# Latent experts weighted by the square root of the gate, and the kept experts with eight buffers

## The reference

```
# layer 0, latent mixture: 32 experts, 8 of them per token
wsel = take(scores, topi); wsel = wsel / wsel.sum(-1) * 2.5
cw = zeros((T, 32)).at[token, topi].add(wsel)       # gate of each token and expert, never negative
x_lat = x @ fc1_w.T                                 # T x 128
h = relu2(einsum('tl,eil->eti', x_lat, w1))         # 32 x T x 128
h = h * cw.T[:, :, None]
routed = einsum('eti,eli->tl', h, w2) @ fc2_w.T
# layer 1, kept experts: 48, each takes at most 96 tokens
gu = einsum('ech,eoh->eco', xb, gate_up_proj); g, u = split(gu)
out = einsum('eci,ehi->ech', silu(g) * u, down_proj)
final = zeros_like(x).at[tok].add(out[...] * w)
```

## Time and profile before

| | |
|---|---|
| time, median of 3 runs | 3288.59 us (3288.56 to 3289.65) |
| the profiled execution | 3292.41 us, of which the span from first to last instruction is 3290.7 us |
| PE, PEld | busy 2926.5 us (89%), 2298.1 us (70%) |
| DVE, ACT, POOL | busy 1834.3 us (56%), 1582.4 us (48%), 704.0 us (21%) |
| DMA | 125.69 MB, 39 GB/s over the span |
| routing phase | 892 to 952 us of the span |
| latent experts | 952 to 1398 us |
| kept experts | 3080 to 3262 us, then the last additions to the end |

### The profile page before, as it was taken

The page is one execution under the profiler, slowest core; times in us unless marked ns, Lnnn a source line. Parts: engine busy times, 40 slices in busy tenths (PEclk is TensorE's granted clock), DMA queues, the critical chain, the costliest instruction groups (busy, mean ns, idle before and its releaser), DMA issues. The chain is left out here.

```text
span 3290.7 us, 52269 instructions
## 1 busy us (share of the span) xinstructions
PE 2926.5 (89%) x17936; PEld 2298.1 (70%) x17936; DVE 1834.3 (56%) x3318; ACT 1582.4 (48%) x2917; POOL 704.0 (21%) x735
## 2 busy tenths in 40 slices
PE   5699999959849999969999999999999999958584
PEld 4544444358737777658888888888888888857453
DVE  5388888451177777755555555555555554555321
ACT  5247777744149999843333333333333333324110
POOL 2412222100120000012222222222222222204564
PEclk7789999979679999979999999999999999965555
DMA  4865554000010000000000000000000000031366
GB/s 148 230 94 79 73 74 67 5 15 0 14 40 0 0 0 0 0 20 10 10 6 3 10 10 10 10 10 10 10 10 10 4 6 10 8 109 56 89 145 125
DMA packets 149298, 125.69 MB, mean 38 GB/s; under 512 B 16960, under 2 KB 134240, under 8 KB 148640
## 3 DMA queue, kind: packets, MB, share of 16 engines
q1 hardware_dynamic: 140752, 109.47, 15.1%
q0 software_dynamic: 8448, 14.99, 2.5%
HBM read 82.55 MB, written 46.06 MB: 39 GB/s over the span
## 5 line engine op out<-in xcount | busy, mean ns | idle before, releaser
L744 DVE TENSOR_REDUCE score_pm<-score_SM 128x1 f32<-128x512 f32 (+3 forms) x608 | 364.5, 658 | 122.8 <-PE score_SM L613 72.9
L1399 POOL TENSOR_TENSOR lin_o2sum<-lin_o2sum,lin_o 128x512 f32<-128x512 f32 x128 | 165.6, 1294 | 1047.3 <-ACT lin_o L1435 1047.3
L704 ACT ACTIVATE score_PR<-score_SE 128x512 f32<-128x512 f32 (+1 forms) x640 | 310.5, 559 | 105.1 <-PE score_SE L638 101.7
L1614 DVE SCALAR_TENSOR_TENSOR lin_go<-lin_gT,lin_O 128x512 f32<-128x512 f32 x128 | 88.0, 688 | 477.7 <-ACT lin_o L1435 477.7
L1470 PE MATMUL lin_PJ<-C_XH,lin_WH 128*128 128x512 f32 x1032 | 341.7, 412 | 13.1 <-DVE lin_WL L1574 13.1
L1470 PE MATMUL lin_PJ<-C_XH,lin_WL 128*128 128x512 f32 x1032 | 320.5, 392 | 0.0
L1470 PE MATMUL lin_PJ<-C_XL,lin_WH 128*128 128x512 f32 x1032 | 320.3, 392 | 0.0
L1418 ACT ACTIVATE lin_qT<-lin_PJ 128x512 f32<-128x512 f32 x129 | 77.2, 598 | 378.3 <-PE lin_PJ L1470 378.3
L1631 DVE TENSOR_TENSOR lin_acc<-lin_OUT,lin_acc 128x512 f32<-128x512 f32 x256 | 177.1, 692 | 140.2 <-PE lin_OUT L1505 138.8
L610 PE MATMUL score_SM<-score_KR,score_QR 96*128 96x512 bf16 (+3 forms) x768 | 230.3, 341 | 27.7 <-DMA score_V<-v_rows 25.0
L1241 DVE TENSOR_TENSOR experts_h<-experts_sq,experts_CW 128x512 f32<-128x512 f32 x256 | 176.2, 688 | 92.7 <-ACT experts_sq L1155 92.6
(11 more groups left out here) (343 smaller groups left out, 6708.4 us busy)
## 6 DMA issues: line engine op xcount, KB each, us to landing
score_QR<-q_parts SPq DMA_DIRECT2D x96, 128.0 KB
score_KR<-k_parts SPq DMA_DIRECT2D x96, 128.0 KB
kept_GU<-L_ffn_gate_up_proj SPq DMA_DIRECT2D x48, 192.0 KB
v_rows<-qkv_vt SPq DMA_DIRECT2D x32, 256.0 KB, 2.6
score_V<-v_rows SPq DMA_DIRECT2D x16, 512.0 KB
C_w<-L_attn_w_qkv SPq DMA_DIRECT2D x51, 128.0 KB, 2.3
q_parts<-qkv_parts SPq DMA_DIRECT2D x16, 384.0 KB, 2.7
k_parts<-qkv_parts SPq DMA_DIRECT2D x16, 384.0 KB, 2.6
```

The lines of the kernel that those rows point to most:

```text
L704: nc.scalar.activation(PR[:, st % BUFS, h, 0:width], SE[:, e % RING, 0:width], ACT.Exp, scale=SCALE)\
L744: nc.vector.tensor_reduce(pm[:, n % 2, h0:h0 + nh, t, k0 // CHUNK], SM[:, count % RING, 0:nh * nk].rearrange("p (h k) -> p h k", h=nh), AX ...
```

## The change

Three parts.

**Roots in place of gates.** Since the gate c is not negative, relu(a)^2 * c = (max(a, 0) * sqrt(c))^2. The routing phase now ends in sqrt(w): a floor at 1e-30, ACT's square root, one Newton step on DVE (a reciprocal, two elementwise operations, and one that also multiplies by the selection mask), 32 fp32 transposes, and a copy. The result (32 x 4096) is stored to a tensor in HBM, `B_roots`. `pick`, its matmul, `CW` and the bf16 parts are gone. In the expert phase SP loads the roots of four experts and one chunk to all 128 partitions at once (`sq`, 128 x 4 x 512 fp32, the source repeated for every partition), four such buffers in turn.

**Another pipeline for the latent experts.** DVE makes z = max(HP, 0) * root in one instruction; ACT squares z twice, once to fp32 and once to fp32r; the low part is made by DVE, and for every fourth expert by POOL. `HP`, `h`, `hh`, `hl` have four buffers, `Y` two (so chunks alternate), the fc2 products are issued behind experts 4 and 7.

**Kept experts.** Eight buffers in place of six, and PE's transposes go one expert further ahead.

The core of the diff (lines that only go away are in the listing above):

```
@@ group_routing_phase @@
-def group_routing_phase(nc, a, scores, CWT, identb, W1H, W1L, W2H, W2L, pick):
+def group_routing_phase(nc, a, scores, roots, ident, W1H, W1L, W2H, W2L):
...
-        TB = ph.ps("TB", [CWR, 4, 1024], BF16)
+        TB = ph.ps("TB", [E, 4, 2 * CHUNK])
...
+            for j in range(4):
+                sp.wait_ge(copied, j + 1)
+                cols = slice(j * 2 * CHUNK, (j + 1) * 2 * CHUNK)
+                sp.dma_start(roots[:, cols], rootT[:, cols]).then_inc(stored, 16)
+            sp.wait_ge(stored, 64)
...
-            nc.gpsimd.memset(pick[:], 0.0).then_inc(zero, 1)
-            pool.wait_ge(zero, 1)
-            for j in range(TERMS):
-                rows = pick[j * E:(j + 1) * E]
...
-            pool.wait_ge(picked, TERMS)
             for n, (w, e) in enumerate(LOADS):
...
-            step(nc.vector.tensor_copy(parts[:, :, 0, :], w[:]))
-            step(tt(rest[:], w[:], parts[:, :, 0, :], ALU.subtract))
-            step(nc.vector.tensor_copy(parts[:, :, 1, :], rest[:]))
-            tt(parts[:, :, 2, :], rest[:], parts[:, :, 1, :], ALU.subtract).then_inc(parts_ready, 1)
+            nc.vector.tensor_scalar(root[:], w[:], 1.0e-30, None, ALU.max).then_inc(positive, 1)
+            dve.wait_ge(rooted, 1)
+            step(nc.vector.reciprocal(inv[:], root[:]))
+            step(tt(inv[:], inv[:], w[:], ALU.mult))
+            step(tt(inv[:], inv[:], root[:], ALU.add))
+            nc.vector.scalar_tensor_tensor(root[:], inv[:], 0.5, left[:], ALU.mult, ALU.mult).then_inc(roots_ready, 1)
...
-            pe.wait_ge(parts_ready, 1)
+            pe.wait_ge(roots_ready, 1)
             for t in range(TILES):
-                ins = nc.tensor.transpose(TB[:, t // 8, (t % 8) * P:(t % 8 + 1) * P],
-                                          parts[:, t].rearrange("p s e -> p (s e)"), identb[:])
+                ins = nc.tensor.transpose(TB[:, t // 8, (t % 8) * P:(t % 8 + 1) * P], root[:, t, :], ident[:])
...
+            act.wait_ge(positive, 1)
+            nc.scalar.activation(root[:], root[:], ACT.Sqrt).then_inc(rooted, 1)
             for j in range(4):
                 act.wait_ge(transposed, j + 1)
-                nc.scalar.activation(CWT[:, j * 1024:(j + 1) * 1024], TB[:, j], ACT.Copy).then_inc(copied, 1)
-
+                nc.scalar.activation(rootT[:, j * 2 * CHUNK:(j + 1) * 2 * CHUNK], TB[:, j], ACT.Copy).then_inc(copied, 1)
@@ experts_phase @@
-    SLOTS = 3
+    QE = 4
+    NQ = E // QE
+    BUFS = 4
+    COPY_AT, OUT_AFTER, ADD_AT = 2, (4, 7), (7, 10)
...
+        sq = ph.sb("sq", [P, BUFS, QE, CHUNK])
+        z = ph.sb("z", [P, 2, CHUNK])
+        h = ph.sb("h", [P, BUFS, CHUNK])
+        hh = ph.sb("hh", [P, BUFS, CHUNK], F32R)
+        hl = ph.sb("hl", [P, BUFS, CHUNK], F32R)
         y = ph.sb("y", [P, CHUNK])
+        HP = ph.ps("HP", [P, BUFS, CHUNK])
+        Y = ph.ps("Y", [P, 2, CHUNK])
         OP = ph.ps("OP", [P, 2, D])
...
+        def on_pool(e):
+            return e % 4 == 3
...
+            def load(g, q):
+                src = roots[q * QE:(q + 1) * QE, bass.ds(g * CHUNK, CHUNK)]
+                sp.dma_start(sq[:, q % BUFS], src.rearrange("(o e) n -> o e n", o=1).to_broadcast([P, QE, CHUNK]))\
+                    .then_inc(sq_in[q % BUFS], 16)
+            for q in range(BUFS):
+                load(0, q)
             sp.dma_start(fc2[:], a["L0_ffn_fc2_w"]).then_inc(w_in, 16)
+            with sp.Fori(0, CHUNKS - 1) as g:
+                for q in range(NQ):
+                    sp.wait_ge(dve_z, done(g * E + q * QE + QE - 1))
+                    load(g + (q + BUFS) // NQ, (q + BUFS) % NQ)
+            def weigh(g, e):
+                n = g * E + e
+                if e % QE == 0:
+                    q = e // QE
+                    dve.wait_ge(sq_in[q % BUFS], 16 * (g * (NQ // BUFS) + q // BUFS + 1))
+                dve.wait_ge(act_hh, done(n - 2))
+                dve.wait_ge(pe_h, done(n))
+                nc.vector.scalar_tensor_tensor(z[:, e % 2], HP[:, e % BUFS], 0.0, sq[:, (e // QE) % BUFS, e % QE],
+                                               ALU.max, ALU.mult).then_inc(dve_z, 1)
+            def low(g, e):
+                n = g * E + e
+                dve.wait_ge(pe_y, done(n - BUFS))
+                dve.wait_ge(act_hh, done(n))
+                nc.vector.tensor_tensor(hl[:, e % BUFS], h[:, e % BUFS], hh[:, e % BUFS].bitcast(F32), ALU.subtract)\
+                    .then_inc(dve_hl, 1)
+            def add(n, g, half):
+                dve.wait_ge(pe_o, done(n))
+                xt = X[:, bass.ds(g * TPC + 2 * half, 2), :]
+                nc.vector.tensor_tensor(xt, OP[:], xt, ALU.add).then_inc(dve_x, 1)
+            with dve.Fori(0, CHUNKS) as g:
+                for e in range(E):
+                    weigh(g, e)
+                    if e and not on_pool(e - 1):
+                        low(g, e - 1)
+                    if e in ADD_AT:
+                        half = ADD_AT.index(e)
+                        add(2 * g + half, (g + CHUNKS - 1) % CHUNKS, half)
...
+        @block.gpsimd
+        def _(pool):
+            give_credit(pool, pool_hl)
+            with pool.Fori(0, CHUNKS) as g:
+                for e in range(3, E, 4):
+                    n = g * E + e
+                    pool.wait_ge(pe_y, done(n - BUFS))
+                    pool.wait_ge(act_hh, done(n))
+                    nc.gpsimd.tensor_tensor(hl[:, e % BUFS], h[:, e % BUFS], hh[:, e % BUFS].bitcast(F32), ALU.subtract)\
+                        .then_inc(pool_hl, 1)
 
...
+            def square(g, e):
+                n = g * E + e
+                act.wait_ge(dve_z, done(n))
+                act.wait_ge(pe_y, done(n - BUFS))
+                nc.scalar.activation(h[:, e % BUFS], z[:, e % 2], ACT.Square).then_inc(act_h, 1)
+                nc.scalar.activation(hh[:, e % BUFS], z[:, e % 2], ACT.Square).then_inc(act_hh, 1)
...
+            with act.Fori(0, CHUNKS // 2) as i:
+                for v in range(2):
+                    g = i * 2 + v
+                    for e in range(E):
+                        square(g, e)
+                        if e == COPY_AT:
+                            copy_y(g, 1 - v)
...
+            def up(g, e, source):
+                n = g * E + e
+                cols = bass.ds(source * CHUNK, CHUNK)
+                s = e % BUFS
+                pe.wait_ge(dve_z, done(n - BUFS))
                 nc.tensor.matmul(HP[:, s], W1H[:, e, :], LH[:, cols], start=True, stop=False)
                 nc.tensor.matmul(HP[:, s], W1H[:, e, :], LL[:, cols], start=False, stop=False)
                 nc.tensor.matmul(HP[:, s], W1L[:, e, :], LH[:, cols], start=False, stop=True).then_inc(pe_h, 1)
 
-                pe.wait_ge(dve_h, done(before(n, e)))
-                nc.tensor.matmul(CW[:, s], pick[:, e, :], CWT[:, cols], start=True, stop=True).then_inc(pe_cw, 1)
-
+            def down(g, v, e):
+                s = e % BUFS
+                if e == 0:
+                    pe.wait_ge(act_y, done(g - 1))
+                pe.wait_ge(act_hh, done(g * E + e))
+                nc.tensor.matmul(Y[:, v], W2H[:, e, :], hh[:, s], start=(e == 0), stop=False)
+                nc.tensor.matmul(Y[:, v], W2L[:, e, :], hh[:, s], start=False, stop=False)
+                if on_pool(e):
+                    pe.wait_ge(pool_hl, done(pool_turn(g, e)))
+                else:
+                    pe.wait_ge(dve_hl, done(dve_turn(g, e)))
+                nc.tensor.matmul(Y[:, v], W2H[:, e, :], hl[:, s], start=False, stop=(e == E - 1)).then_inc(pe_y, 1)
 
             def out(n, half):
+                if half == 0:
+                    pe.wait_ge(act_y, done(n // 2))
                 pe.wait_ge(dve_x, done(n - 1))
...
+            with pe.Fori(0, CHUNKS // 2) as i:
+                for v in range(2):
+                    g = i * 2 + v
+                    for e in range(E):
+                        to = g + (e + AHEAD) // E
+                        up(to, (e + AHEAD) % E, to % CHUNKS if v and e + AHEAD >= E else to)
+                        down(g, v, e)
+                        if e in OUT_AFTER:
+                            half = OUT_AFTER.index(e)
+                            out(2 * g + half, half)
...
@@ kept_experts_phase @@
-SLOTS = 6
+SLOTS = 8
...
-            def first(i, u):
+            def gathered(i, u):
 
                 pe.wait_ge(g_in[u], (i + 1) * 16)
                 turn(i * S + u, u)
+            def weighed(i, u):
                 pe.wait_ge(w_in[u], (i + 1) * 32)
                 products(i * S + u, u)
 
 
-            first(0, 0)
+            gathered(0, 0)
+            gathered(0, 1)
+            weighed(0, 0)
             with pe.Fori(0, KEPT // S - 1) as i:
                 for u in range(S):
-                    first(i + (u + 1) // S, (u + 1) % S)
+                    gathered(i + (u + 2) // S, (u + 2) % S)
+                    weighed(i + (u + 1) // S, (u + 1) % S)
                     outputs(i * S + u, u)
             for u in range(S):
 ```

(14 more changed lines are left out.)

147 lines of the change are left out of this document (38 added, 109 removed).

## The result

Four runs of the changed kernel took 3231.82 us in the median (3229.2 to 3234.89), four of the kernel before beside them 3288.62. The ratio is 0.9825, 95% interval 0.9813 to 0.9837: 57 us faster, of 68 forecast. The profiled execution took 3233.19 us (span 3231.4; before, 3290.7).

What follows compares the result with a forecast made beforehand. PE was taken to bound the latent experts, ACT close behind. Routing with store +6.4, start +11.7, latent loop -66.6 and kept experts -19.5 sum to -68.0 us: 3220 us from the median 3288.6, range 3200 to 3258.

Steps and rivals of the forecast that it cites:

- Latent loop, -66.6: Latent experts, steady part: without the pick matmul a chunk takes 45.9 us, 8.3 less, over eight chunks -66.6 us.
- the sign that was to show the prediction wrong in its core: Latent loop: the prediction is wrong in its core if PE waits inside the loop after the first chunk.
- What its chain through ACT's squares takes: Latent loop, DVE: z, squares, low part and hand-overs take 1.3 to 1.4 us per expert, close under PE's 1.38.
- Start of the phase, +11.7: Before the latent loop: fc2 queues behind four loads of roots at 306 GB/s, +9.7 us, plus 2 for PE's restart.
- the upper bound that I had written down: Start of the latent phase: at most +27 us, with the four loads at 146 GB/s taking 28.7 us.
- The 2 us that I had added for the low clock: Start of the latent loop: PE restarts at the lower clock level after standing some ten us, estimated at 2 us.
- Routing up to the last copy, +4.1: Routing phase: added DVE and ACT work net +9.0 us, POOL's selects gone -9, fp32 transposes +4.1.
- Kept experts, -19.5: Kept experts: pace from 3.47 to POOL's 2.98 us, -22.8, against +1.3 for the first products and +2 for uneven laps.
- The loads partly hold the loop: Rival, latent loop: root loads at 165 GB/s stretch the phase to 414 us in place of 385, 3249 us; chance 0.08.
- Slower than before: Rival, latent loop: root loads at 146 GB/s take 460 us, making the kernel slower, 3302 us; chance 0.10.
- DVE held by POOL: Rival, latent loop: POOL's low parts slow DVE's, 5.8 us per four experts against PE's 5.5, 3250 us; chance 0.09.
- The kept experts keep their pace: Rival, kept experts: waits for the earlier scatter or the gather's landing grow, no gain there, 3241 us; chance 0.13.

Runs made afterwards that it cites:

- experiment 4: Changed kernel, with each load of roots after the first four filling only one partition of 128; 3226.01 us, ratio 0.9811.
- experiment 10: Changed kernel with fc2 loaded ahead of the roots and roots in chunk order, plus all low parts on DVE; 3202.42 us, ratio 0.9732.
- experiment 2: Changed kernel with the roots in chunk order in HBM, a load's four rows following each other; 3208.95 us, ratio 0.9758.
- experiment 11: Changed kernel with the memset and three selects put back on GpSimd at the start of the routing phase; 3244.98 us, ratio 0.9856.

## Why the prediction was right, and where not

**Right in sign and nearly in size** (forecast 3220, measured 3231.8, inside the range). That the total came so near is in part luck: one step missed by 12 us, and the terms for routing and kept experts came out 5 us better than forecast. By its own steps, forecast against trace:

**Latent loop, -66.6: -64.0.** PE was bound by six matmuls at 0.227 us, a chunk takes 45.3 where nothing disturbs it, and the hand-over is gone (experiment 4; 45.9 forecast). The 2.6 us short are the loads' 5.7 (371.2 against 365.5 without them), less 3.1 by which the forecast was too careful (435.2 - 66.6 = 368.6 against 365.5). Still, the sign that was to show the prediction wrong in its core did come: PE waits inside the loop after the first chunk. It costs some 6 us of 371, so the step stands, but the statement that PE alone sets the pace holds only without the roots' loads. DVE never was the pace: with all low parts its own work is 1.20 us per expert, since an operation of 0.68 holds it for 0.60 (experiment 10). What its chain through ACT's squares takes, 1.3 to 1.4 by the forecast, was not measured apart.

**Start of the phase, +11.7 (and +2.3 for the store): +25.9. This step failed.** The order of events was as forecast: PE waits for fc2, fc2 for four loads ahead of it. The rate was not. I priced the loads at 306 GB/s, the rate of a row in which the engines move other data another way; that row's transfers are stores of zeros into HBM, as the DMA issues of that stretch in the trace of before show (KB, us to landing):

```profile
odd_sums<-rank_zero SPq DMA_DIRECT2D x1, 4128.0 KB, 19.3
```

The first load to fc2's landing took 29.4 us, which is 147 GB/s. That is the rate of the upper bound that I had written down from the earlier trace rows and set aside. With the roots next to each other the same step took 13.4 us, 323 GB/s (experiment 2), where the forecast had 15.6. So the mechanism and the arithmetic were right, and what the sum had wrong was the rate of loads in which all partitions read the same rows 16 KB apart. (The 2 us that I had added for the low clock fall into the loop by this split. At a granted clock of 0.50 the first seven steps of its matmuls are 0.43 to 0.59 us in place of 0.227, 1.6 us more in all.) The Trainium skill, page "DMA: Bandwidth & Descriptors", section "Latency and other measured facts", reports that copies with a row pitch of a large power of two lose much of their rate, and that a few KiB of padding restore it. Its figures are for pitches from 512 KiB on, with private rows for each partition. The runs here agree with the remedy (2 KB of padding sufficed) and show the loss at 16 KB, for shared rows only.

**Routing up to the last copy, +4.1: +0.7.** Without POOL's selects beside DVE -10.3 in place of -9 (from the phase's first instruction to the end of the 32 MAX8 operations 38.6 us before, 28.3 now; experiment 11 takes it back), the added operations from the floor on 12.2 in place of 13.0 with the reciprocal at 6.55 as against 6.7, transposes and copies +2.6 in place of +4.1, since a transpose with 32 columns to load takes 0.20 us where one with 128 took 0.245.

**Kept experts, -19.5: -21.3** (scatters -22.6, first one +0.5, way out +0.8). POOL was next at 2.98 as forecast, and with eight buffers alone PE's 3.19 was met to the hundredth.

**The rivals.** The loads partly hold the loop: this happened, but at 5.7 us and not 29, because they ran at 173 to 183 GB/s from chunk to chunk, and not at 165, against the 185 that PE can use. Slower than before: its 146 GB/s was met (147), but only at the start, where nothing else ran and the loads came all at once. In the middle of the loop they run at up to 183; why the start is slower than the middle was not tried. DVE held by POOL: no. The 192 low parts on DVE took 0.69 us in the median and 0.78 at most. Only 12 of them met one of POOL's (1.30 us long), for 0.23 us at most, and took at most 0.09 us longer, where the rival had priced 1.0 for each of 64. POOL's fell beside z, for 0.65 us in the median, and z took 0.69 us there and 0.68 in experiment 10, where POOL does nothing. So the rival priced meetings that hardly happen, and DVE alone would do. The kept experts keep their pace: no, scatters are 2.99 apart.

## What to carry to other kernels

A load's rate is a matter of its pattern in memory: price it from a row of the same direction, piece and pitch, and where there is none, keep the slow row in the sum and not in the margin. When many partitions read the same few rows, lay these rows next to each other, and issue a small load that the first instructions need ahead of the large ones. Where a loop goes round through two engines and two transfers, count how many steps share the lap before moving work earlier: one of two edits that are good together cost 52 us alone. Whether an engine can take more work is read from how far its starts are apart where work waits for it, not from durations.

## What the runs showed of the hardware

Broadcast loads of four rows to 128 partitions: rows 16 KB apart nearly fill the engines (share 0.9 to 1.0) at 173 to 183 GB/s and move 147 at the start; 18 KB or 2 KB apart 186 GB/s cost a share of 0.50 or 0.51, and the start moves 323 with rows 2 KB apart. DVE starts operations of 0.68 us every 0.60 us. z, which reads one input from PSUM and one from SBUF, takes 0.69 us beside POOL's subtraction and 0.68 without it. A reciprocal costs DVE 6.4 ns per element of a partition, 6.55 us for 1024, over five times a multiplication of that size (1.22). A DVE maximum of two SBUF inputs, 512 elements, took 4.20 us under GpSimd's select and 0.69 without.
